# Two graph layers on one core: x1 kept turned in the order of the values, q and k projections reading in steps of 16 bytes

## The reference, cut to what matters

```
x: 32 graphs x 512 nodes x 512 features; adj: 512 x 512, about 3% of it set
layer 0:  h = x @ W (512 -> 256);  e = leaky_relu(h.a0 + (h.a1)^T);  e masked by adj;  alpha = softmax(e)
          x1 = layernorm(x + concat(alpha @ h, h))
layer 1:  q = x1 @ Wq.T + bq;  k = x1 @ Wk.T + bk;  v = x1 @ Wv.T + bv     (8 heads of 64)
          S = q k^T / 8, masked by adj;  A = softmax(S);  o = A v
          out = layernorm(x1 + o @ Wo.T + bo)
```

## Time and profile before

| | us |
|---|---|
| median of 3 runs (lowest, highest) | 3135.08 (3133.39, 3146.21) |
| the profiled execution, its own time | 3133.3 |
| its span, first to last instruction | 3131.5 |
| TensorE matmuls busy | 2970.1 (95%) |
| VectorE busy | 2670.4 (85%) |
| ScalarE busy | 2445.5 (78%) |
| GpSimd busy | 2040.9 (65%) |

### The profile page before, as it was taken

How to read it: one execution, slowest core, us unless ns; L and a number is a source line. 1 busy time by engine, 2 the same in 40 slices (tenths; PEclk the granted TensorE clock), 3 DMA queues, 4 the chain that set the end, 5 groups by cost and what they waited for, 6 DMA issues and landing times.

```text
span 3131.5 us, 58284 instructions
## 1 busy us (share of the span) xinstructions
PE 2970.1 (95%) x19084; PEld 2504.4 (80%) x19084; DVE 2670.4 (85%) x6556; ACT 2445.5 (78%) x5031; POOL 2040.9 (65%) x1415
## 2 busy tenths in 40 slices
PE   4899999999999999999999999999999999999995
PEld 4788888887888887888888888888888888888874
DVE  5888888888888888888888888888888888888874
ACT  4777888777888777888777888778887778887764
POOL 1566676666766667666667666666766666766664
PEclk8999999999999999999999999999999999999997
DMA  3566676666766666666666666666666666666664
GB/s 124 199 217 219 231 242 220 216 219 216 241 231 219 219 218 226 231 234 216 220 222 220 233 233 221 216 219 230 231 229 216 218 220 231 242 219 218 213 207 159
DMA packets 306413, 685.39 MB, mean 219 GB/s; under 512 B 56896, under 2 KB 90432, under 8 KB 273344
## 3 DMA queue, kind: packets, MB, share of 16 engines
q1 hardware_dynamic: 306112, 681.68, 63.5%
HBM read 375.40 MB, written 306.18 MB: 218 GB/s over the span
## 4 chain that ended last, share of the span: by engine, by line
PE 71%; DVE 14%; issue 7%; ACT 5%; DMA 1%; POOL 1%; DVEq 0%; SPq 0%; ACTq 0%; POOLq 0%
PE R_bank L729 41%; PE O_bank L818 11%; PE S_bank L799 9%; PE L_bank L729 6%; PE L_bank L720 4%; DVE blocked L1115 3%; DVE stats L995 3%; DVE prob L1095 2%; DVE tokens L1083 2%; ACT qk_pair L859 1%; DVE o_half L1123 1%; DVE alpha L1040 1%; DVE x1T L991 1%; DVE qk_pair L1012 1%; ACT alpha L891 1%
## 5 line engine op out<-in xcount | busy, mean ns | idle before, releaser
L1175 POOL TENSOR_TENSOR turned_lo_prob<-turned_lo_prob,turned_hi_prob 128x1024 fp32r<-128x1024 f32 x512 | 1250.2, 2459 | 539.1 <-ACT turned_hi_prob L846 539.0
L934 ACT ACTIVATE prob<-prob,small_cols 128x512 f32<-128x512 f32 x1024 | 730.8, 715 | 228.8 <-DVE small_cols L1095 222.3
L1115 DVE STREAM_TRANSPOSE blocked<-prob 128x512 f32<-128x512 f32 x1024 | 696.4, 697 | 113.9 <-PE O_bank L818 59.4
L1095 DVE CUSTOM_DVE_ANT_0 prob<-S_bank,mask 128x512 f32<-128x512 f32 x1024 | 678.3, 681 | 35.5 <-PE S_bank L799 31.2
L846 ACT ACTIVATE turned_hi_prob<-turned_lo_prob 128x1024 fp32r<-128x1024 f32 x512 | 528.1, 1050 | 46.0 <-PE O_bank L818 29.8
L818 PE MATMUL O_bank<-turned_hi_prob,v_st 128*128 128x256 f32 x2048 | 521.7, 292 | 38.4 <-POOL turned_lo_prob L1175 38.3
L818 PE MATMUL O_bank<-turned_lo_prob,v_st 128*128 128x256 f32 x2048 | 507.6, 285 | 0.0
L799 PE MATMUL S_bank<-qk_pair 64*128 64x512 f32 x3072 | 444.8, 414 | 22.6 <-DVE small_cols L1095 19.7
L818 PEld LDWEIGHTS O_bank<-turned_hi_prob,v_st 128*128 128x128 f32 x2048 | 394.3, 193 | 79.2 <-POOL turned_lo_prob L1175 63.2
L729 PE MATMUL R_bank<-wv,x1T 128*128 128x256 f32 x3072 | 401.3, 286 | 0.2
L818 PEld LDWEIGHTS O_bank<-turned_lo_prob,v_st 128*128 128x128 f32 x2048 | 395.5, 193 | 4.2
(11 more groups left out here) (90 smaller groups left out, 4445.7 us busy)
## 6 DMA issues: line engine op xcount, KB each, us to landing
scratch<-blocked SPq DMA_DIRECT2D x256, 1024.0 KB, 4.1
turned_lo_prob<-scratch SPq DMA_DIRECT2D x256, 1024.0 KB, 5.6
tokens<-xT SPq DMA_DIRECT2D x128, 256.0 KB, 5.1
tokens<-x SPq DMA_DIRECT2D x128, 256.0 KB, 3.1
r_wide<-r_scratch SPq DMA_DIRECT2D x512, 64.0 KB, 3.4
out<-tokens SPq DMA_DIRECT2D x128, 256.0 KB, 4.1
r_scratch<-r_cols SPq DMA_DIRECT2D x256, 16.0 KB
tokens<-adj SPq DMA_DIRECT2D x1, 1024.0 KB, 6.8
```

What stands on the lines that cost most here:

```text
L934: act.activation(prob_tile(R, s), prob_tile(R, s), ACT.Exp, bias=negmax[:, slot:slot + 1], scale=-1.0, accum_out=psum_row[:, ph % 2, j:j + ...
L1095: dve.tensor_tensor_reduce(prob_tile(R, s), score_bank(R, s)[:, :], mask[:, s % 8 // 2, :], -SCALE, HUGE, ALU.add, ALU.min, negmax[:, slot ...
L1115: dve.transpose(blocked[:, ph % 2, :, :, 2 * (s % 2) + s % 4 // 2, :].rearrange("p d c i -> p c d i"), prob_tile(R, s).rearrange("p (d c i ...
L1175: pool.tensor_tensor(lo_ap, lo_ap.bitcast(F32), turned_hi_prob[:, 2 * a:2 * a + 2, :, :].bitcast(F32), ALU.subtract).then_inc(p_lo, 1)
```

## The change

x1 is kept in `x1T` in another order within each tile of 128 tokens: place 4j+d holds token 32d+j (j from 0 to 31, d from 0 to 3). ScalarE and VectorE read the bank of the transposes in this order (`token_of_place`: steps of 32 fp32 numbers, four times, in the innermost dimension) and write `x1T` contiguously. The q and k projections read `x1T` in token order (`by_token`), which is in steps of four fp32r numbers, 16 bytes. V and W take the tile as it lies, so the rows of v are in place order. Keys, mask, and the columns of S are in token order, so the eviction of k is like that of q, the mask is built and read contiguously, and `vt` reads its tile by 32 contiguous numbers in the order c, d in place of d, c. No instruction is added or removed, no plan is changed, and no wait.

```diff
-        def turned_keys(columns):
-            return columns.rearrange("p (d m) -> p d m", d=4)
-        def by_key_place(columns):
-            return columns.rearrange("p (m d) -> p d m", d=4)
+        def by_token(columns):
+            return columns.rearrange("p (c j d) -> p c d j", c=T, d=4)
+        def token_of_place(columns):
+            return columns.rearrange("p (c d j) -> p c j d", c=C, d=4)
+        def placed(part):
+            return part.rearrange("p c (j d) -> p c j d", d=4)
...
-                    project(ring(R, name)[:, :], lambda s, c: w[:, s, c, c0:c0 + P], lambda m, c: x1T[:, m, c, :],
+                    project(ring(R, name)[:, :], lambda s, c: w[:, s, c, c0:c0 + P], lambda m, c: by_token(x1T[:, m, c, :]),
                             ring_mm)
...
-                    if kind == "k":
-                        hi_ap, bank_ap = turned_keys(hi_ap), by_key_place(bank_ap)
                     act.activation(hi_ap, bank_ap, ACT.Identity, bias=b_col[:, pair % 4:pair % 4 + 1]).then_inc(qk_hi, 1)
...
-                    split_hi(x1T[:, HI, :, i * P:(i + 1) * P], solo_bank(name)[:, :].rearrange("p (c t) -> p c t", c=C), solo_hi)
+                    split_hi(placed(x1T[:, HI, :, i * P:(i + 1) * P]), token_of_place(solo_bank(name)[:, :]), solo_hi)
...
-                    if kind == "k":
-                        lo_ap, hi_ap, bank_ap = turned_keys(lo_ap), turned_keys(hi_ap), by_key_place(bank_ap)
                     dve.scalar_tensor_tensor(out=lo_ap, in0=bank_ap, scalar=b_col[:, pair % 4:pair % 4 + 1],
...
-                    by_node = al.rearrange("p (m d) -> p m d", d=4)
-                    dve.tensor_tensor_reduce(by_node, by_node, mask[:, i, :].rearrange("p (d m) -> p m d", d=4),
-                                             -1.0, HUGE, ALU.add, ALU.min, a_negmax[:, i:i + 1]).then_inc(a_red, 1)
+                    dve.tensor_tensor_reduce(al, al, mask[:, i, :], -1.0, HUGE, ALU.add, ALU.min, a_negmax[:, i:i + 1]).then_inc(a_red, 1)
...
-                    split_lo(x1T[:, LO, :, i * P:(i + 1) * P], solo_bank(name)[:, :].rearrange("p (c t) -> p c t", c=C),
-                             x1T[:, HI, :, i * P:(i + 1) * P], solo_done)
+                    split_lo(placed(x1T[:, LO, :, i * P:(i + 1) * P]), token_of_place(solo_bank(name)[:, :]),
+                             placed(x1T[:, HI, :, i * P:(i + 1) * P]), solo_done)
...
                 dve.transpose(blocked[:, ph % 2, :, :, 2 * (s % 2) + s % 4 // 2, :].rearrange("p d c i -> p c d i"),
-                              prob_tile(R, s).rearrange("p (d c i) -> p c d i", c=T, i=BLK)).then_inc(p_turned, 1)
+                              prob_tile(R, s).rearrange("p (c d i) -> p c d i", c=T, i=BLK)).then_inc(p_turned, 1)
...
-                dve.tensor_scalar(turned_keys(mask[:, t, :]), by_key_place(tokens[2][:, t, :].bitcast(I32)), 0.0, MASKED,
+                dve.tensor_scalar(mask[:, t, :], tokens[2][:, t, :].bitcast(I32), 0.0, MASKED,
                                   ALU.is_equal, ALU.mult).then_inc(mask_built, 1)
```

## The result

The kernel after took 3747.38 us (median of 4, 3745.6 to 3749.05) against 3134.23 before: 1.1952 times, 95% interval 1.1938 to 1.1967. The forecast was 3775. The profiled execution's span is 3745.0 us.

The account below looks back on a forecast made before the run. TensorE was taken as the bound, matmuls busy 95% of the span. 3133.3 us plus 694 for stepped q and k reads, minus 50 of waits and 4 for the mask builder, made 3773, or 3775 beside the median; range 3100 to 3850.

Parts of the forecast that it names:

- Part 1: q and k matmuls on TensorE: the 16-byte step adds a second column time, 226 ns each for 3072, +694 us.
- The upper end from the mask builder: q and k matmuls: worst case, 2.9 ns more a column, 4.6 ms in all, from the builder's 3.35 ns an element.
- Parts 3, 4 and 5: Evictions of k, evictions of x1T (597 and 690 ns) and the `vt` turnings (697 ns): no change expected.
- Part 6: Building the mask with contiguous reads: 4 us less, once; ends 0 and 6.
- Part 2: VectorE's first-layer reductions, mask read contiguously: floor 1066 to about 684 ns; at most 34 us if TensorE has time.
- the waits: TensorE's waits for GpSimd, q and k, and minima, 86.6 us in all: 50 us taken away; x1T's stays.
- the sum: Whole kernel: 3133.3 + 694 - 50 - 4 = 3773 us, or 3775 beside the median; a graph about 116 us.
- most of the standing goes: TensorE in each graph: with 21.7 us more work, most of its 2.5 us of standing disappears.
- The signs: Profile after: q and k groups 5.5 us apart, graph 115 us, other engines 65 to 75%, reduction floor near 690 ns.
- The first rival: TensorE doesn't feel the step and VectorE's relief arrives: 3095 to 3112 us, likeliest 3107; chance 0.33.
- The second rival: TensorE doesn't feel the step and the relief is not seen, reductions' time being GpSimd's interference: 3118 to 3150 us; chance 0.15.

Follow-up runs that it names:

- e1: Kernel before, with only the moving operand of the q and k projections read in steps of 16 bytes: 3763.38 us, ratio 1.1998.
- e4: Kernel before, each projection's moving operand in another step (8 to 512 bytes, pairs, contiguous): 452 ns a matmul at 8 bytes, 464 at 16, 540 at 512.
- e14: Kernel before, moving operands in new runs, gaps and turns through 16-byte pieces: 328, 282, 457, 260 ns a matmul for runs and pairs, 216, 478, 466 for turns.
- e7: Kernel after, with the mask read in steps of 256 bytes again in the first layer's reductions: 3764.33 us, ratio 1.2003.
- e2: Kernel after, with q and k reading x1T contiguously, all other parts of the change kept: 3095.83 us, ratio 0.9868.
- e11: Kernel after, with q and k reading x1T contiguously and their evictions from PSUM putting the order right: 3110.36 us, ratio 0.9923.

## Why the prediction was right

**Part 1, a second column time for each column:** right, and in size: 226 ns more for each of 3072 matmuls were forecast, and 225 measured as the mean of the eight projections, 691 against 694 us. e1 shows that it is the whole loss. The mechanism (a stepped read of SBUF slows TensorE, one of PSUM doesn't slow ScalarE and VectorE) came from the right rows. The size was in good part luck. VectorE's 382 to 418 ns are 0.75 to 0.82 ns an element on 1.3 (684 / 512), so six tenths of an element and not "about as much again". Taken as a share they would have given 390 to 450 us, taken in ns about 1200, and "a second column time" is a round number between them that no row gave. VectorE's SBUF rows also pointed to SBUF and not to the step of 16 bytes. The halving is not special to 16 bytes; 8 bytes would have cost the same. The upper end from the mask builder was worthless: of its 3.35 ns an element only 0.43 (218 ns / 512) were the step.

The Trainium skill (Advanced Engine Details and Errata, Memory Cachelines) gives SBUF lines of 16 bytes and asks for two hits in a line. The pieces of 16 bytes agree with e4 to e14. For a moving fp32r operand two hits give half speed (452 ns against 234), and it takes all four; for 128 stationary columns behind a matmul of 256 two are enough (120 ns). The sentence of the Trainium skill (SBUF — State Buffer, in the section on the DMA port swizzle) that calls strides up to four fp32 numbers free is contradicted by 464 ns at four.

**Parts 3, 4 and 5:** right. The evictions of k, those of x1T (597 to 598, 690 to 691 ns) and the turnings (697 ns) didn't move; PSUM took steps of 16 and 128 bytes for nothing.

**Part 6:** the builder gained 218 ns in each of 4, 0.9 us where 4 were taken. The builder was priced at the 684 ns of a contiguous reduction, and without its steps it takes 1498.

**Part 2 and the waits, the 28 us between forecast and result:** the sum took 50 us of waits away and had no term for VectorE's relief. e1 against before is +627 us where the columns alone are +691, so without the relief the waits gave 64 and not 50. From start to start, a graph in mid-run is 19.80 us longer in e1: 21.58 more in the eight projections, 0.63 less behind N, where TensorE waited for GpSimd, 1.21 less around D0, where it waited for the eviction of q2 and k2, and 0.09 more before the scores, where it waits for the minima. In 31 graphs these come to 54 us; the rest lies in small pieces and at the ends. (The profile's busy time gives only 44 us of standing less in e1; in it the ends of matmuls are modelled.) And the relief wasn't worthless: e7 puts 16 to 17 us on it. 14 + 16 + 3 (225 for 226 ns) - 3 (the builder) = 30. So "most of the standing goes" was right for GpSimd and for q and k, and wrong for the minima, which the sum had among the waits that go: in e1 this wait is 22.4 us (19.7 before). It hangs on red0, which runs while TensorE has nothing else to do, and a slower projection elsewhere doesn't give it time; only the contiguous mask does.

**The signs:** PEld, VectorE and ScalarE fell to 68, 69 and 65%, as forecast; GpSimd fell to 53%, outside the 65 to 75. A graph takes 113.90 us, where the sum said 116 in one place and the signs 115 in another: 92.0 + 21.7 makes 113.7 with all standing gone. The floor of the reduction is 649 ns and not near 690, which was read from the median of L1095 (684); its shortest, 648, was the row for a floor.

**The first rival** was sized 17 to 34 us and a few for the mask builder; e2 shows 41, of which 35 in the two waits it named (34 was its upper end). The second rival, that the reductions' time is GpSimd's and not the stride's, falls with the floor of 649 ns, and its time, 3118 to 3150 us, with the 3096 of e2.

## What to carry to other kernels

When columns have to change their order, do it where PSUM is read: there steps of 16 and 128 bytes were free for ScalarE and VectorE (if the order fits into one instruction; in e11 VectorE needed four), while the step of 16 bytes in SBUF doubled the column time of TensorE and added 0.4 us to a reduction of 512 on VectorE. Before moving a stride onto an engine, ask which engine has none to give: the change took 0.4 us from four VectorE instructions in a graph and gave 0.225 us to 96 TensorE instructions. Read the price of a stride from an instruction that has it and one that hasn't, of the same operation; a single slow instruction with a stride in it is no price. And relief on an engine that isn't the bottleneck is worth something where the bottleneck waits for just that instruction: of the four reductions in a graph one paid, by the timelines of e1 and the kernel after.

## What the runs showed of the hardware that was not expected

TensorE's moving fp32r operand costs about 1.8 ns for each new aligned piece of 16 bytes, at 2.4 GHz, and hardly more than 0.9 ns a column up to steps of 64 bytes: 234 ns for 512 contiguous columns (0.25 pieces each), 260, 282 to 286 and 328 to 348 for 0.28, 0.31 and 0.375, 452 to 457 for 0.5, and 432 to 464 for 0.75 and 1. Turning through eight pieces took 478 ns and a step of 512 bytes 540, both above this ceiling, and why isn't known. Runs of four aligned numbers with gaps are as fast as contiguous ones, and a piece that comes back after one other is free.

Contiguous fp32r columns don't run at TensorE's best speed. A number read twice took 216 ns for 512 columns, 0.42 ns each, and so did a walk to and fro between two pieces; four times took 223 and step 0 225 in the two slower places. Each is 18 to 19 ns less than a contiguous read in the same place. The walk to and fro needs as many pieces as a contiguous read, so the count of pieces alone doesn't explain it.

The stationary operand has the same 1.7 to 1.8 ns a piece with no ceiling up to 128 pieces, hidden up to the length of the matmul before. Why the moving operand has the ceiling wasn't tried.
